# Rows of a graph layer by matmuls over 64 partitions, two chunks side by side in the halves of the array

## The reference

```
q = h @ Wq + bq;  k = h @ Wk + bk;  v = h @ Wv + bv
eh = edge_features @ We + be
hmid = leaky_relu(concat(q[src], k[tgt], eh) @ A1 + b1)
scores = leaky_relu(hmid @ A2 + b2)
w = softmax(scores.mean(-1), axis=0)
out = segment_sum(w[:, None] * v[tgt], src)
x + layernorm(h @ Wn + bn + out) * gamma + beta
```

## Time and profile before

| what | value |
|---|---|
| median of 3 runs | 6913.11 us (6894.9 to 6924.62) |
| span of the profiled execution | 5409.9 us |
| the profiled execution's own time | not listed; median less span is 1503.2 us |
| granted TensorE clock, mean | 0.956 |
| busy: TensorE, DVE, GpSimd, ACT | 84%, 76%, 59%, 51% |
| DMA | 1288.10 MB, mean 238 GB/s |

### The profile page before, as it was taken

The page is one execution under the profiler, slowest core; times in us unless marked ns, Lnnn a source line. Parts: engine busy times, 40 slices in busy tenths (PEclk is TensorE's granted clock), DMA queues, the critical chain, the costliest instruction groups (busy, mean ns, idle before and its releaser), DMA issues. The chain is left out here.

```text
span 5409.9 us, 144289 instructions
## 1 busy us (share of the span) xinstructions
PE 4556.7 (84%) x35867; PEld 3650.3 (67%) x35867; DVE 4104.4 (76%) x11137; ACT 2745.2 (51%) x6463; POOL 3207.3 (59%) x3405
## 2 busy tenths in 40 slices
PE   8656566888888888889989989999999699889988
PEld 3544445666666666777777777777777477788888
DVE  7655555777777777777887877878877577899998
ACT  5333333444444444555555555555555233677777
POOL 3777777777777777777777777777777200000000
PEclk9888788999999999999999999999999899999999
DMA  6788867888888877787887887887877588999998
GB/s 210 186 252 255 253 190 219 264 263 259 269 262 263 250 208 212 225 243 234 242 242 234 243 241 234 245 239 236 244 238 231 172 219 222 247 259 258 264 266 232
DMA packets 1964810, 1288.10 MB, mean 238 GB/s; under 512 B 638970, under 2 KB 1857185, under 8 KB 1964700
## 3 DMA queue, kind: packets, MB, share of 16 engines
q1 hardware_dynamic: 1780245, 838.11, 59.6%
q0 software_dynamic: 154752, 435.99, 21.6%
q10 hardware_dynamic: 29704, 12.84, 0.9%
HBM read 716.22 MB, written 570.23 MB: 238 GB/s over the span
## 5 line engine op out<-in xcount | busy, mean ns | idle before, releaser
L1219 POOL DMA_INDIRECT slots<-rows,slot_i x3224 | 3115.8, 966 | 993.1 <-issue 912.4
L1275 PE MATMUL ps_row<-win,mixed 128*128 128x256 f32 x5840 | 1537.1, 409 | 291.5 <-ACT rows L1363 274.0
L1275 PEld LDWEIGHTS ps_row<-win,mixed 128*128 128x128 f32 x5840 | 1107.0, 202 | 491.1 <-ACT rows L1363 329.0
L1363 ACT ACTIVATE rows<-ps_row 128x512 f32<-128x512 f32 x1460 | 883.0, 605 | 122.3 <-PE ps_row L1275 121.6
L1360 ACT ACTIVATE rows<-lo_all 128x8 f32 (+1 forms) x403 | 87.2, 216 | 1525.7 <-DMA slots<-rows,slot_i 1525.7
L823 ACT ACTIVATE low<-ps_z 128x512 f32<-128x512 f32 x882 | 534.4, 606 | 534.7 <-PE ps_z L755 308.0
L1246 PE MATMUL ps_e<-ident,edges 128*128 128x128 f32 x3224 | 516.9, 286 | 290.7 <-ACT mixed L1352 189.5
L1246 PEld LDWEIGHTS ps_e<-ident,edges 128*128 128x128 f32 x3224 | 420.0, 148 | 459.9 <-ACT mixed L1352 206.4
L851 DVE TENSOR_TENSOR mid<-low,ps_z 128x512 f32<-128x512 f32 x882 | 604.2, 685 | 163.8 <-ACT low L823 121.1
L755 PE MATMUL ps_z<-onehot,q_bits 128*128 128x512 bf16 x2646 | 721.0, 382 | 0.4 <-DVE onehot L842 0.4
L842 DVE TENSOR_SCALAR onehot<-ps_ls,part 128x512 bf16<-128x512 bf16 x654 | 314.8, 481 | 355.9 <-ACT raised L796 179.4
(11 more groups left out here) (214 smaller groups left out, 6404.8 us busy)
## 6 DMA issues: line engine op xcount, KB each, us to landing
u_rows<-slots SPq DMA_DIRECT2D x1176, 258.0 KB, 3.4
edges<-edge_attr_dram SPq DMA_DIRECT2D x403, 256.0 KB
v_own<-slots SPq DMA_DIRECT2D x392, 258.0 KB, 3.8
q_bits<-qb_tab SPq DMA_DIRECT2D x882, 96.0 KB, 3.2
slots<-no_row SPq DMA_DIRECT2D x98, 528.0 KB
slots<-rows,slot_i POOLq DMA_INDIRECT x3224
early_v<-slots SPq DMA_DIRECT2D x196, 258.0 KB
slots<-no_row SPq DMA_DIRECT2D x98, 396.0 KB
```

Of the source, the lines that this page charges most:

```text
L1219: pool.indirect_dma_start(slots_tab[h], bass.IndirectOffsetOnAxis(slot_i[:, u, j:j + 1], 0), rows[:, u, j, :], None).then_inc(scattered[u] ...
L1275: last = pe.matmul(bank[:, j % 2, :], mixed[:, u % 2, j, :], win[:, u, :], start=True, stop=True)
L1363: nc.scalar.activation(rows[:, u, 2 * k:2 * k + 2, 0:2 * U0].rearrange("p j (a c) -> p j a c", a=2)[:, :, :, 0:D], row_bank(s, k).rearrang ...
```

## The change

Edge features and one-hot no longer share a tile. Features go to `feats` (contiguous, 64 numbers an edge), and one transpose turns two chunks together: the even chunk's features land on partitions 0 to 63, the odd one's on 64 to 127 (`featT`). The one-hot is now made already turned: ACT copies the window offsets of a group to bf16 (`copy_rel`), TensorE spreads each chunk's offsets over 64 partitions of `ps_rel`, and DVE compares them with the partition's number (`pickT`). The window is loaded twice, into both halves of the partitions of `win`. Each chunk's rows are then two matmuls over 64 partitions that add up in PSUM: `pickT` x `win` (256 columns) and `featT` x `w2` (128 columns). Even and odd chunks alternate between the halves of the array and between two banks; a bank now holds chunks j and j + 2 (`chunks_of`). `ps_e` shrinks to one bank and is turned and copied once a group.

```diff
         def load_edges(s, u):
             if at_least(s, UNROLL):
-                wait_turned(sp, s - UNROLL, 1)
+                sp.wait_ge(edges_turned, s - (UNROLL - 1))
-            sp.dma_start(edges[:, u, :, 0:DE], edge[bass.ds(e0, GE), :]...)
+            sp.dma_start(feats[:, u, :, :], edge[bass.ds(e0, GE), :]...)
         def load_window(s, u):
-            sp.dma_start(win[DE:P, u, :], kv_tab[bass.ds(row, WIN), :]).then_inc(win_in[u], 16)
+            for b in range(2):
+                sp.dma_start(win[b * WIN:(b + 1) * WIN, u, :], kv_tab[bass.ds(row, WIN), :]).then_inc(win_in[u], 16)
...
-        def turn_half(s, u, b):
-            if b == 0:
-                pe.wait_ge(edges_in[u], count(s, u, 16))
-                pe.wait_ge(onehot_ready, s + 1)
-            if at_least(s, 1):
-                pe.wait_ge(feats_ready, s * 2 + (b - 1))
-            for k in range(HALF):
-                last = pe.transpose(ps_e[:, b, k, :], edges[:, u, b * HALF + k, :], ident[:])
+        def turn(s, u):
+            pe.wait_ge(edges_in[u], count(s, u, 16))
+            pe.wait_ge(rel_ready, s + 1)
+            if at_least(s, 1):
+                pe.wait_ge(feats_ready, s)
+                pe.wait_ge(pick_ready, s)
+            for k in range(HALF):
+                pe.transpose(ps_e[:, k, :], feats[:, u, 2 * k:2 * k + 2, :]..., ident[:])
+            for j in range(PER):
+                lo = WIN * (j % 2)
+                last = pe.matmul(ps_rel[lo:lo + WIN, j // 2, :], rel_b[:, u, j:j + 1].to_broadcast([P, WIN]), ident_b[:],
+                                 is_transpose=True, start=True, stop=True)
+            last.then_inc(edges_turned, 1)
...
-            for j in (2 * k, 2 * k + 1):
-                last = pe.matmul(bank[:, j % 2, :], mixed[:, u % 2, j, :], win[:, u, :], start=True, stop=True)
-            last.then_inc(rows_made, 1)
+            for j in range(HALF):
+                lo, at = WIN * (j % 2), row_bank(s, 2 * h + j % 2)[:, j // 2, :]
+                pe.matmul(at, pickT[lo:lo + WIN, u % 2, 2 * h + j // 2, :], win[lo:lo + WIN, u, :],
+                          start=(j < 2), stop=False, skip_group_check=True)
+            for j in range(HALF):
+                lo, at = DE * (j % 2), row_bank(s, 2 * h + j % 2)[:, j // 2, D:2 * D]
+                op = pe.matmul(at, featT[lo:lo + DE, u % 2, 2 * h + j // 2, :], w2[lo:lo + DE, :],
+                               start=False, stop=True, skip_group_check=True)
+                if j >= 2:
+                    op.then_inc(rows_made, 1)
...
+        def copy_rel(s, u):
+            act.wait_ge(hot_ready, s + 1)
+            nc.scalar.activation(rel_b[:, u, :], rel_all[:, bass.ds(s, 1), :]..., ACT.Copy).then_inc(rel_ready, 1)
-        def copy_feats(s, u, b):
+        def copy_feats(s, u):
...
         def one_hot(s, u):
-            nc.vector.tensor_tensor(edges[:, u, :, DE:P], iota_p[:, 0:WIN]..., rel_all[:, bass.ds(s, 1), :]...,
-                                    ALU.is_equal).then_inc(onehot_ready, 1)
+            dve.wait_ge(edges_turned, s + 1)
+            nc.vector.tensor_scalar(pickT[:, u % 2, :, :], ps_rel[:], part[:, 2:3], None, ALU.is_equal).then_inc(pick_ready, 1)
```

More of the change, by code:

```diff
@@ L259, in gnn_layer @@
             first_in = sem("first_in")
-            N_FILLED = 14
+            N_FILLED = 13
             N_MADE = N_FILLED + 13
@@ L293, in _ @@
                     nc.gpsimd.memset(ones_b[:], 1.0).then_inc(made, 1)
-                    nc.gpsimd.memset(win[:], 0.0).then_inc(made, 1)
                     nc.gpsimd.memset(ok_i[:], 0).then_inc(made, 1)
@@ L579, in weights_of @@
                         nc.vector.tensor_copy(wm[:, 3 * D:4 * D], ps_w[:, 1, D:2 * D]).then_inc(ready, 1)
-                        nc.vector.tensor_copy(w2[:], ps_w[:, 1, 2 * D:3 * D])
-                        for u in range(UNROLL):
-                            op = nc.vector.tensor_copy(win[0:DE, u, D:2 * D], ps_w[0:DE, 1, 2 * D:3 * D])
-                        op.then_inc(ready, 1)
+                        nc.vector.tensor_copy(w2[:], ps_w[:, 1, 2 * D:3 * D]).then_inc(ready, 1)
                         nc.vector.tensor_copy(bias[:, D:2 * D], ps_w[:, 0, 0:D])
@@ L994, in early_row @@
                 return place_of(q % 2, b)[1]
[L996 to L1001 removed]
             def wait_ranked(eng, s):
                 if known(s) and s == 0:
[L1006 removed]
+                    eng.wait_ge(begun, 1)
                 else:
@@ L1217, in scatter @@
                             pool.sem_inc(passed, 1)
-                            for j in (2 * k, 2 * k + 1):
+                            for j in chunks_of(k):
                                 pool.indirect_dma_start(slots_tab[h], bass.IndirectOffsetOnAxis(slot_i[:, u, j:j + 1], 0),
@@ L1260, in rank, with make_rows @@
                         return last
-                    def make_rows(s, u, k):
-                        if k == 0:
-                            pe.wait_ge(win_in[u], count(s, u, 16))
-                        if k % 2 == 0:
-                            pe.wait_ge(feats_ready, s * 2 + (k // 2 + 1))
-                        if before_scores(s):
-                            if at_least(s, 1):
-                                pe.wait_ge(row_done, s * HALF + (k - 3))
-                        else:
-                            pe.wait_ge(row_done, s * HALF + (k - 1))
-                        bank = row_bank(s, k)
-                        for j in (2 * k, 2 * k + 1):
-                            last = pe.matmul(bank[:, j % 2, :], mixed[:, u % 2, j, :], win[:, u, :], start=True, stop=True)
-                        last.then_inc(rows_made, 1)
+                    def make_rows(s, u, h):
+                        if h == 0:
+                            pe.wait_ge(win_in[u], count(s, u, 32))
+                            pe.wait_ge(feats_ready, s + 1)
+                            pe.wait_ge(pick_ready, s + 1)
+                        if not before_scores(s):
+                            pe.wait_ge(row_done, s * HALF + 2 * h)
+                        elif at_least(s, 1):
+                            pe.wait_ge(row_done, s * HALF + (2 * h - 2))
+                        for j in range(HALF):
[8 more added lines that the diff above has]
+                                op.then_inc(rows_made, 1)
@@ L1278, in step @@
                     def step(s, u):
-                        turn_half(s + 1, (u + 1) % UNROLL, 0)
+                        turn(s + 1, (u + 1) % UNROLL)
                         make_rows(s, u, 0)
+                        rank(s + 1, (u + 1) % UNROLL)
                         make_rows(s, u, 1)
-                        turn_half(s + 1, (u + 1) % UNROLL, 1)
-                        rank(s + 1, (u + 1) % UNROLL)
-                        make_rows(s, u, 2)
-                        make_rows(s, u, 3)
@@ L1315, in both @@
                         if more:
-                            turn_half(s + 1, v, 0)
+                            turn(s + 1, v)
                         make_rows(s, u, 0)
-                        make_rows(s, u, 1)
                         for n in units[:late]:
@@ L1334, in _ @@
                     with pe.If(flag):
-                        turn_half(0, 0, 0).then_inc(begun, 1)
-                        turn_half(0, 0, 1)
+                        turn(0, 0)
                         rank(0, 0).then_inc(begun, 1)
@@ L1363, in copy_rows @@
                         nc.scalar.activation(
-                            rows[:, u, 2 * k:2 * k + 2, 0:2 * U0].rearrange("p j (a c) -> p j a c", a=2)[:, :, :, 0:D],
+                            rows[:, u, chunks_of(k)[0]:chunks_of(k)[1] + 1:2, 0:2 * U0].rearrange("p j (a c) -> p j a c", a=2)[:, :, :, 0:D],
                             row_bank(s, k).rearrange("p j (a c) -> p j a c", a=2), ACT.Copy).then_inc(row_done, 1)
@@ L1975, in gnn_layer @@
         weighed = mask_chain
-        x_made = sem("x_made")
-        x_copied = sem("x_copied")
-        added = sem("added")
-        f_in = sem("f_in")
-        f_chain = sem("f_chain")
-        f_out = sem("f_out")
+        x_made = o.one_ready
+        x_copied = o.low_ready
+        added = o.mid_ready
+        f_in = o.raised_ready
+        f_chain = o.kept_ready
+        f_out = o.scored
         with nc.Block() as block:
```

72 lines of the change are left out of this document (35 added, 37 removed).

## The result

The change makes the kernel slower: 7174.26 us (7165.38 to 7198.55, 4 runs) against 6904.0 us for the kernel before in the same rounds, a ratio of 1.0399 with a 95% interval of 1.0373 to 1.0425. The forecast was 6912 us and a range up to 6990, so the time lies above it.

The account below looks back on a forecast made before the run. GpSimd's scatters were taken to bound the kernel, hiding all other changes, so the 5409.9 us span stayed 5410; with 1503.2 us carried over from span to timed median this gave 6912 us, range 6870 to 6990.

Parts of the forecast that it names:

- the last of the sum: Outside the profiled span: 1503.2 us between span and timed median, carried over unchanged onto 5410 us to give 6912 us.
- GpSimd's queue never runs dry, and it sets the pace: Stage of scatters: GpSimd bounds 4100 of 5409.9 us, at 1.27 us a scatter, 10.1 to 10.2 us a group; chance 0.78.
- TensorE, 0.3 us a group less with pairing: TensorE's work per group: 3.95 us added against 4.23 removed if half-row passes pair, leaving 8.9 us.
- the sign that I had named: TensorE's trace: pairing would show as starts a few ns apart on the two halves of the array.
- half-row passes do not run side by side: Row matmuls: without pairing TensorE does 2.48 us more a group and becomes the bound, 7044 to 7311 us; chance 0.10.
- ScalarE's wait for scatters grows from 3.7 us: ScalarE before overwriting `rows`: 0.39 us less copying a group, so its 3.7 us wait for scatters grows.
- All these are priced at nothing, under the cover of GpSimd: Per-group changes on TensorE, ACT, DVE, SyncE and DMA: zero cost or gain while each stays under GpSimd's 10.15 us.
- Its new waits on both copies: Before the first rows: TensorE's turn of group 1 waits for both copies, putting rows near 146 us.
- The rival on the slow side: Stage of scatters: TensorE takes over as bound because half-row passes do not pair, 7044 to 7311, middle 7180 us; chance 0.10.
- The start: Up to the first scatter: 0 to +2 us from later rows, 0 to -2 us from a shorter prologue, taken as 0.

Follow-up runs that it names:

- a_no_pairs: The changed kernel with the four chunks of a half in the order 0, 2, 1, 3 on both runs of row matmuls: 5404.35 us, ratio 1.0.
- a_window_once: The changed kernel with one window load, the other half of `win` zeroed once: 5401.52 us, ratio 0.9995 to the kernel before.
- a_ranked: The changed kernel with VectorE's `wait_ranked` on a semaphore of its own: 5405.81 us, ratio 1.0003; on a slow chip 7180.65 us, ratio 1.04.
- a_window_one_dma: The changed kernel with both halves of the window filled by one DMA, its source read twice: 5410.01 us, ratio 1.0013 to the kernel before.

## Why the prediction was wrong

*The failed step is the last of the sum:* "between its span and the median of the three runs, 6913.11, lie 1503.2 us, which I carry over". I took the two numbers as one execution and its surroundings. Around a span lie 1.8 us (7165.38 against 7163.6). The runs show no such 1503.2 us around any execution. They were stalls in the very stage that the change touches, so none of the profile's free margins held in the timed runs. A profile 22% below the timed runs bounds nothing about them.

*"GpSimd's queue never runs dry, and it sets the pace"* holds for the profiled chip, and the near relatives of the changed kernel (`a_no_pairs`, `a_window_once`, `a_ranked`, `a_window_one_dma`) stay at 5402 to 5410 us on chips of that kind, as that step says. The changed kernel itself never came onto one. Where it was timed the step is false: 1175.6 us of GpSimd's idle time belong to ScalarE before the change and 1609.2 after it.

*TensorE, 0.3 us a group less with pairing:* right. In the late part of a chip of 5.40 ms it is busy 1304.86 / 1500 x 10.14 = 8.82 us a group in `a_window_once`, against 9.19. Eight one-hot passes take 1.13 us and eight feature passes 0.61 (at 3004.38 and 3005.34 us above), 1.57 us from the start of the one to the end of the other, where the eight full passes took 1.89. In the trace of `a_window_once` the passes start in pairs 7 ns apart, the sign that I had named, and the one-hot pairs follow at 0.216 us, which is the pace of single passes before. So the rival "half-row passes do not run side by side" is wrong, and TensorE is no bound.

*ScalarE's wait for scatters grows from 3.7 us:* wrong in direction, with nothing of the sum resting on it. In `a_no_pairs` it is 514.7 us in 177 groups, 2.9 us, because 189.6 us of its slack went into a new wait of `copy_rel` for VectorE's `hot`.

*"All these are priced at nothing, under the cover of GpSimd"* was the consequence. I named the cover, and had no price for the case that it is gone. With it gone the load costs 0.9%, TensorE's order 0.7%, ScalarE's place 1.8% more. "Its new waits on both copies" appear in the prediction only for the start.

*The rival on the slow side* named TensorE, with 7044 to 7311 us. The measured 7174 lies within it, 6 us from its middle of 7180, by luck and not by its mechanism: TensorE's busy share fell from 77% to 67% of 2800 to 3900 us.

*The start:* the first scatter begins at 147.48 us against 145.86, within the 0 to +2 that I gave.

## What to carry to other kernels

Before a row of a profile is used, set its span against the timed runs; where they differ by more than a per cent or so, the difference is itself the first thing to explain, and the sum has to be made a second time for a kernel whose cover is gone. An engine's program order is free only while every update it waits for comes promptly: put a wait behind work that is ready, and let it share an update that is waited for anyway, as the old place of the copy did. A rearrangement that joins two small handoffs into one at the start of a step should be priced as one more place for all engines to stand.

## What the runs showed of the hardware

- The kernel before took 5404 us on three chips and 6827 to 6914 us on three others (medians), with nothing in between, and its executions on each stayed within 1% of the median. One alone did not: 9640.11 us, one of 31 on a chip of 5404 us, and nothing here explains it. ScalarE's, VectorE's and GpSimd's instructions last the same on both (a scatter 964 to 966 ns). What differs is when updates arrive, in the stage of scatters alone: the last stage takes 1162 to 1170 us everywhere, and outside the stage of scatters no late update is recorded. In the records of that stage, SyncE's register and semaphore instructions, some 0.03 us on the one kind, take over 0.5 us about 1080 times in 6820.9 us on the other, once on the first. Why a chip is of one kind is open.
- Matmuls on two halves of the rows paired in either order in the program: with (0, 2, 1, 3) in place of (0, 1, 2, 3) eight one-hot passes took 1.14 us against 1.13, and eight feature passes 0.71 against 0.61.
- TensorE's granted clock was lower where it stalled: 0.81 to 0.87 in stretches where late updates came, 0.96 to 0.99 in like stretches where none did. Its work per group is then longer, 10.0 us busy at 0.85 (736.70 us in 589 / 8 groups) against 8.8 at 0.97, yet it is still idle a third of the time, so the clock is not the bound here.
